# Wide Householder columns: the product with x by TensorE in fp32, panel additions during the wait, no unread streams

## What is computed

```python
# x: (16, 512, 128), adj: (512, 512)
h = einsum('bnd,ed->bne', x, fc_in_w) + fc_in_b
for _ in range(8):                                   # "Euler steps"
    h = h + dt * (alph * 0.5 * (adj @ h - h) + h @ w_eff - h + x)
x = layernorm(x + h)
deg = A.sum(0) + A.sum(1) - diag(A)                  # A = adj
L_norm = rsqrt(deg)[:, None] * (diag(deg) - A) * rsqrt(deg)[None, :]
_, U = eigh(L_norm)
out = relu((U.T @ x) @ W1 + b1) @ W2 + b2
x = layernorm(x + U @ out)
```

## Time and profile before

| | us |
|---|---|
| three runs | 3918.97, 3944.32, 3945.27 |
| median | 3944.32 |
| span of the profiled execution | 3918.1 |

### The profile page before, as it was taken

One profiled execution on the slowest core, in us unless ns is written; L12 is line 12 of the kernel. 1 busy time (PEld: TensorE's weight loads), 2 busy tenths in 40 slices (PEclk: granted clock), 3 DMA queues, 4 the chain that ended last, 5 costly groups with the idle time before them and its releaser, 6 DMA issues.

```text
span 3918.1 us, 62251 instructions
## 1 busy us (share of the span) xinstructions
PE 2790.1 (71%) x13749; PEld 2130.1 (54%) x13749; DVE 3270.7 (83%) x19331; ACT 1093.6 (28%) x4884; POOL 841.7 (21%) x4216
## 2 busy tenths in 40 slices
PE   7999999999999999889999777772123242140088
PEld 6677777777767767667677666662022221020043
DVE  6888999999889888788877777778889999989924
ACT  2333333333333344344444333321000010000013
POOL 3242222222222222233322344440000000000000
PEclk8988999999999999898888655555556566565599
DMA  2000000000000000000000000000000000000001
GB/s 64 1 1 1 1 2 1 1 2 2 1 1 2 1 1 2 1 6 1 1 1 1 1 1 1 1 1 27 1 1 0 0 1 0 0 0 0 0 0 43
DMA packets 14584, 17.39 MB, mean 4 GB/s; under 512 B 1664, under 2 KB 11008, under 8 KB 13952
## 3 DMA queue, kind: packets, MB, share of 16 engines
q1 hardware_dynamic: 14208, 13.42, 1.1%
HBM read 9.22 MB, written 4.19 MB: 3 GB/s over the span
## 4 chain that ended last, share of the span: by engine, by line
DVE 46%; PE 41%; issue 7%; ACT 3%; POOL 3%; DVEq 0%; DMA 0%; POOLq 0%
PE ps L684 10%; PE ps L723 7%; DVE h L2102 4%; PE ps L777 3%; PE ps L640 3%; PE ps L710 3%; PE ps L654 2%; PE ps L662 2%; PE ps L702 2%; DVE small L1613 2%; DVE ps L1597 2%; DVE small L1603 2%; DVE small L1535 2%; PE ps L980 1%; ACT UR L1280 1%
## 5 line engine op out<-in xcount | busy, mean ns | idle before, releaser
L684 PE MATMUL ps<-ident 128*128 128x256 f32 x2992 | 820.9, 414 | 0.0
L684 PEld LDWEIGHTS ps<-ident 128*128 128x128 f32 x2992 | 566.1, 203 | 67.7 <-issue 6.4
L723 PEld LDWEIGHTS ps<-UR 128*128 128x128 f32 x2552 | 378.2, 212 | 195.6 <-DVE UR L1670 93.1
L723 PE MATMUL ps<-UR 128*128 128x41 f32 (+17 forms) x2552 | 390.8, 285 | 95.1 <-ACT UR L1280 69.6
L1068 POOL TENSOR_SCALAR small<-small 128x1 f32<-128x1 f32 x511 | 117.4, 230 | 1227.3 <-ACT small L1244 1209.4
L1242 ACT ACTIVATE small<-ps 128x1 f32<-128x1 f32 x511 | 87.4, 171 | 705.7 <-PE ps L723 705.7
L1264 ACT ACTIVATE small<-lower,small 128x1 f32<-128x1 f32 x383 | 112.9, 295 | 589.3 <-DVE small L1617 589.3
L777 PEld LDWEIGHTS ps<-small,ones 128*128 128x128 f32 x766 | 122.8, 199 | 267.3 <-DVE am L1634 253.7
L702 PE MATMUL ps<-UR,ident 128*128 128x18 f32 (+2 forms) x1020 | 231.6, 309 | 44.3 <-DVE UR L1599 44.3
L1280 ACT ACTIVATE UR<-ident,UR,small 128x1 f32<-128x1 f32 x510 | 197.1, 386 | 99.6 <-POOL small L1077 99.6
L777 PE MATMUL ps<-small,ones 128*128 128x2 f32 x766 | 150.5, 266 | 103.6 <-DVE am L1634 98.1
(11 more groups left out here) (621 smaller groups left out, 7601.7 us busy)
## 6 DMA issues: line engine op xcount, KB each, us to landing
out<-xs SPq DMA_DIRECT2D x16, 256.0 KB, 2.3
m<-in_adj SPq DMA_DIRECT2D x1, 1024.0 KB, 5.4
before<-c_before SPq DMA_DIRECT2D x1, 1024.0 KB, 4.7
notafter<-c_notafter SPq DMA_DIRECT2D x1, 1024.0 KB, 8.2
sib<-c_sib SPq DMA_DIRECT2D x1, 448.0 KB, 3.0
own<-c_own SPq DMA_DIRECT2D x1, 384.0 KB, 3.3
iota<-c_iota SPq DMA_DIRECT2D x1, 256.0 KB, 2.7
h<-c_lanes SPq DMA_DIRECT2D x1, 186.0 KB, 2.4
```

What stands on the lines that cost most here:

```text
L684: nc.tensor.matmul(ps[1][:, 0:2 * P].rearrange("p (a d) -> p a d", a=2), ident[:, 0:P], ident[:, 0:P].unsqueeze(1).broadcast_to([P, 2, P]) ...
L723: last = nc.tensor.matmul(ps[2][:, 0:2 * npend + 3], over(x_of(j)), flat[:, j, 2 * first:2 * k + 3], start=(j == tp), stop=(j == T - 1))
```

## The change

- In wide columns `tile_product` forms the product on TensorE: for each tile m of the result, one fp32 matmul a tile j, with a 128 x 128 block of the matrix as weights and x's one column as the moving operand, summed in `ps[3][:, 16 + m]`. That is `n_on` squared matmuls a column. They stand behind the dots and the s sum; the pivot row goes before the last tile's. `transpose` of x, `row_ready`, VectorE's passes and `y0` go.
- ScalarE copies the products beside VectorE's multiplied pairs, and one reduction (`summed`) gives y. The next matrix column is made in the same way, with its parts copied by ScalarE early, in the time before cy. VectorE writes both halves of the next pair at once (`uc2`, `tcol2`, `pair_masks`), so that ScalarE's two copies at the head of the column go.
- The panel's product is taken over whole tiles into three banks in turn, and VectorE's additions (`panel_rests`) stand just before its wait for the products.
- `keep_clock` keeps two streams at two places in columns 0 to 7 and none from there on. Euler units: one behind cy with four tiles; one behind the products and one behind cy with three tiles outside the panel's columns and with two tiles; one behind cy in the panel's columns with three. So counted, 119 + 208 + 224 = 551, the last in column 366.
- The norms begin at column 390 and come two a column. The table `own` is loaded after the reduction. A, Vt, junk, eye, leafsel and iota become parts of one tensor `big`.
- Narrow columns are a function of their own with the same operations; the pivot row's correction stands ahead of `next_reflected`.

The diff, cut to its core:

```diff
-NORMS_FROM = 292
+NORMS_FROM = 390
-STREAMS = {4: (2, 3, 5), 3: (2, 2, 4), 2: (0, 0, 1), 1: (0, 0, 0)}
-BY_TENSOR = 5
+NORMS_AT_ONCE = 2
...
-            wanted = (1, 0, 1) if n_on > 2 else (0, 1, 1) if n_on == 2 else (0, 0, 0)
-            extra = (0, STREAMS[n_on][place], 0)
+            wanted = (0, 1, 1) if n_on == 2 or n_on == 3 and not panel else (0, 0, 1)
+            extra = (0, 0, 0)
             if k < 8:
+                wanted, extra = (0, 0, 0), (0, 2, 2)
...
+                def tile_product(m):
+                    for j in range(tp, T):
+                        last = nc.tensor.matmul(ps[3][:, 16 + m:17 + m], parts[current[k]][:, j, m * P:(m + 1) * P],
+                                                x_of(j), start=(j == tp), stop=(j == T - 1))
+                    return last
...
                 pe.wait_ge(x_ready, k + 1)
-                if n_on > 1:
-                    for j in range(tp, T):
-                        last = nc.tensor.transpose(ps[0][:, j * P:(j + 1) * P], over(x_of(j)), ident[:, 0:P])
-                    last.then_inc(row_ready, 1)
-                for _ in range(euler_units(k)[0]):
-                    next(state, None)
-                if n_on > 1:
-                    keep_clock(halves_of[k][0])
-                if k <= narrow_from:
-                    pe.wait_ge(xm_ready, k + 1)
-                    if k:
-                        pe.wait_ge(zq_ready, k)
+                if k and k <= narrow_from:
+                    pe.wait_ge(zq_ready, k)
                 if k:
                     pe.wait_ge(u_ready, k)
                 for j in range(tp, T):                      # the dots
...
+                if n_on > 1:
+                    if k:
+                        reflected_product(k - 1)
+                    if switched:
+                        pe.wait_ge(panel_rest, rest_number[first, panel_at[first][2] - 1])
+                    for m in range(tp, T - 1):
+                        tile_product(m)
+                    pivot_row()
+                    tile_product(T - 1).then_inc(products_ready, 1)
...
                 if n_on > 1:
                     pe.wait_ge(y_ready, k + 1)
                     nc.tensor.matmul(ps[3][:, 8:10], ones[:, :], CY, start=True, stop=True).then_inc(cy_ready, 1)
-                    pivot_row()
...
+                        nc.scalar.activation(MBS, pair_masks[:, tp + special, :], ACT.Copy, scale=INVB).then_inc(mb_ready, 1)
+                        act.wait_ge(products_ready, k + 1)
+                        nc.scalar.activation(am[:, 0:n_on * width].rearrange("p (t l) -> p t l", t=n_on)[:, :, 2 * npend:width],
+                                             ps[3][:, 16 + tp:16 + T].unsqueeze(2),
+                                             ACT.Copy).then_inc(product_parts_ready, 1)
                         act.wait_ge(y_done, k + 1)
...
+            def wide_column(k):
+                dve.wait_ge(x_ready, k + 1)
                 if k:
                     next_reflected(k - 1)
+                    reflected_dot(k - 1)
+                inverse = inverse_root(k)
...
+                if npend:
+                    dve.wait_ge(pivot_row_ready, k)
+                    has_column = products(on, n_on, first, npend, ps[4], am[:, 216:432])
+                    h_.wait(has_products)
+                panel_rests(k)
+                dve.wait_ge(product_parts_ready, k + 1)
+                summed(y[:, here], n_on, npend, am[:, 0:216]).then_inc(y_done, 1)
+                dve.wait_ge(y_done, k + 1)
+                h_.post(tt(CY[:, 1:2], y[:, 0:1], ident[:, pp:pp + 1], ALU.mult))
+                h_.sync()
+                stt(out=am[:, 504:504 + n_on], in0=y[:, here], scalar=1.0, in1=x_now,
+                    op0=ALU.mult, op1=ALU.mult, accum_out=CY[:, 0:1]).then_inc(y_ready, 1)
```

More of the change, by code:

```diff
@@ L432, in eig_gnn @@
             n_on, panel = window_of(k)[1], panel_stage(k)
-            place = (0 if panel[1] == 0 else 1 if panel[1] < 2 + panel[4] else 2) if panel else 2
-            wanted = (1, 0, 1) if n_on > 2 else (0, 1, 1) if n_on == 2 else (0, 0, 0)
-            extra = (0, STREAMS[n_on][place], 0)
[L436 to L440, removed]
+            wanted = (0, 1, 1) if n_on == 2 or n_on == 3 and not panel else (0, 0, 1)
+            extra = (0, 0, 0)
             if k < 8:
-                units = (0, 0, 0)
+                wanted, extra = (0, 0, 0), (0, 2, 2)
             left = EULER_UNITS - sum(sum(u) for u in units_of)
[L444 to L447, removed]
+            units_of.append(wanted if left >= sum(wanted) else (0, 0, left))
             halves_of.append(extra)
@@ L452, in euler_units, with norms_at @@
             return units_of[k]
[L454 to L464, removed]
+        SCALES_AT = NORMS_FROM + 2 * T * B // NORMS_AT_ONCE + 4
+        LAST_SCALED = SCALES_AT + 4 + T * B // NORMS_AT_ONCE
+        def norms_at(k, place):
+            if NORMS_FROM <= k < SCALES_AT - 4 or SCALES_AT + 4 <= k < LAST_SCALED:
+                return 1
+            return int(k == SCALES_AT - 4 and place == 0)
         Mrow, AH = before, notafter
@@ L1225, in euler, with pair_mask, panel_copy @@
                             yield
+            def pair_mask(k):
+                tp, n_on, pp = window_of(k)
+                if pp < P - 1:
+                    nc.scalar.activation(pair_masks[:, tp, :], lower[:, pp:pp + 2][:, ::-1], ACT.Copy).then_inc(masks_ready, 1)
+                else:
+                    nc.scalar.activation(pair_masks[:, tp + 1, 0:1], lower[:, 0:1], ACT.Copy).then_inc(masks_ready, 1)
+            def panel_copy(k, what):
+                stage = panel_stage(k)
+                if not stage:
+                    return
+                kb, step, index, t0, n0 = stage
+                i = step - 1
+                if (kb, what, i) not in copied_number:
+                    return
+                cols = slice(t0 * P, N)
+                act.wait_ge(panel_ready, ready_number[kb, i])
+                nc.scalar.activation(panel_rows[i][:, cols], ps[5][0:2 * PANEL, cols], ACT.Copy).then_inc(panel_copied, 1)
@@ L1246, in _ @@
                     nc.scalar.activation(NA[:, 2:5], ps[2][:, 0:3], ACT.Copy).then_inc(root_ready, 1)
[L1247 to L1251, removed]
+                if norms_at(k, 0):
+                    next(norms)
                 if final:
@@ L1462, in _ @@
             for j in range(T):
[L1463 removed]
+                c.post(stt(out=whole[:, j, :], in0=whole[:, j, :], scalar=half[:, j:j + 1],
                            in1=ps[0][:, :], op0=ALU.mult, op1=ALU.mult))
@@ new lines, in _, with products @@
+            h_.post(tt(pairs[:, 0, 0, 0:1], whole[:, 0, 0:1], lower[:, 1:2], ALU.mult))
+            h_.post(stt(out=pairs[:, 0, 0, 1:2], in0=whole[:, 0, 0:1], scalar=lower[:, 0:1], in1=sparks[:, 1, 1:2],
+                        op0=ALU.mult, op1=ALU.add))
+            h_.sync()
+            nc.vector.memset(NOTE, 0.0).then_inc(x_ready, 1)
+            def products(tiles, n_on, first, npend, bank, space):
+                width = 2 * npend + 1
+                swapped = bank[:, 0:2 * npend].rearrange("p (l s) -> p l s", s=2)[:, :, ::-1]
+                mine = space[:, 0:n_on * width].rearrange("p (t l) -> p t l", t=n_on)
+                return h_.mark(tt(mine[:, :, 0:2 * npend].rearrange("p t (l s) -> p t l s", s=2), pairs[:, tiles, first:first + npend, :],
+                                  swapped.unsqueeze(1).broadcast_to([P, n_on, npend, 2]), ALU.mult))
@@ L1527, in reflected_dot @@
                         op0=ALU.mult, op1=ALU.mult, accum_out=SPART).then_inc(z_ready, 1)
-            narrow_from = next(k for k in range(N) if window_of(k)[1] == 1)
-            state = {"panel": 0, "added": 0}
+            state = {"added": 0}
             def half_dot(k):
@@ L1668, in householder @@
                 dve.wait_ge(ucn_ready, k + 1)
-                if not wide_now:
-                    stt(out=pairs[:, tp, k + 1, :], in0=ucN[:, 0:2], scalar=TMP, in1=tcol[:, 0:2],
-                        op0=ALU.mult, op1=ALU.subtract).then_inc(x_ready, 1)
-                    return
                 dve.wait_ge(t_ready, k + 1)
```

444 lines of the change are left out of this document (231 added, 213 removed).

## The result

| | us |
|---|---|
| changed kernel, median of 4 runs | 5383.88 (5374.11 to 5405.14) |
| kernel before, beside it | 3931.64 (3917.99 to 3945.27) |
| ratio, 95% interval | 1.369 (1.3627 to 1.3752) |
| span of the profiled execution | 5378.7 |

The change makes the kernel 37% slower, and 5365 was forecast. The page has VectorE busy 2788 us where it was 3271, and TensorE 4223 where it was 2790. The new product (line 721) is its costliest group; its 7392 weight loads are busy 1581 us, one almost directly behind the other.

A forecast was written before the change was run, and what follows sets the result against it. VectorE's passes over A set the column. Low-clock TensorE products replace them: 3918 + 806 (four tiles) + 475 (three) + 164 (two) = 5363, given as 5365 us; range 4900 to 5600.

The forecast's parts named there:

- The clock: TensorE in wide columns: without streams and with one-column products, the granted clock falls to near 0.50; chance 0.77.
- the first rival: Wide columns keep the full clock: 7.9, 5.8 and 4.7 us a column, 4118 us in all; chance 0.06.
- The price of a record: Each TensorE record, two per fp32 matmul, costs 0.2135 us at the low clock, 0.125 at the full one.
- the rivals: Full clock kept, 4118 us (0.06); mixed clock, about 4740 us (0.12); loads hidden, faster or level, down to 3415 us (0.04).
- A and B: Four-tile column: cy load to next dots, mean 2.0 us; then dots to products, 44 records in order on TensorE, 9.71 us.
- C: Products to cy load, through ScalarE's copy and VectorE's reduction: 1.05, 1.0 and 0.95 us with four, three and two tiles.
- Panel's columns: Panel matmuls, 1.9 us for 480 columns, against 1.3 us of slack: 0.2, 0.1 and 0.1 us a column.
- The clock won back by two units: Columns with two Euler units: full clock 10% of the time in 80 three-tile columns, 30% in 112 two-tile ones.
- What was costed at nothing: Panel additions, one-tile operations, moved norms, ScalarE's tcol activations and the later table load lie under cover and add 0 us.
- The panel additions: VectorE's additions in wide columns lie in the products' shadow: nothing; without that cover at most 44 us.
- the table `own`: Loaded after the reduction, landing in 3.3 us before first need 8 us after the last root: nothing; without cover 3 us.
- VectorE: Its four, three or two passes a wide column leave the chain; it idles before the new reduction, waiting for TensorE's products.

The follow-up runs named there:

- experiment 1: Changed kernel with each new product's moving operand widened from one column: 4288.66 us with 112 columns, 5382.16 with 32, 5234.28 with 64.
- Experiment 2: Kernel before, without unread streams from column 8 on, all else kept: 4445.31 us.
- experiments 1 and 4: The second of the two: changed kernel with four-tile Euler units behind the products instead of behind cy: 5422.4 us, ratio 1.3858.
- experiment 3: Changed kernel with only the diagonal block in each tile's product, 4, 3 and 2 matmuls instead of 16, 9 and 4: 4851.95 us.
- first run of experiment 5: Kernel before, with unread streams in the one-tile stage too, one ahead of the pivot row and two behind cy: 3943.46 us, ratio 1.0067.

## Why the prediction was right, by its steps

The mechanism came out as forecast. That the total lies within 0.4% of 5365 is in part luck: the four- and three-tile stages came out 63 us shorter than forecast and the two-tile stage 74 us longer.

- *The clock.* Right, and what decided: 0.51 to 0.55 in all wide stages, and experiment 1 shows it as the cause. Of the 1452 us lost, 1095 come back when 112 columns move and the rest of the kernel stays; the first rival, the same structure at the full clock, was put at 4118 us and measured at 4289 with a clock of 0.90, 0.94 and 0.85. Experiment 2 shows that taking out the streams is enough to lose much of the clock; the changed kernel with its streams kept was not run, so how much of its low clock is due to them and how much to the new product stays open. By the Trainium skill (TensorE: Matmul & The Clock Gate, section "What's actually happening") the clock follows how busy the engine has been; these runs do not agree if busy means occupied, since TensorE was busy 1514 of 1603 us at 0.51, and they do if it means moving operands.
- *The price of a record.* 0.2135 at the low clock held: 0.213 from one load to the next. At the full clock it is 0.112, not 0.125, and the row of line 600 already said so: the last record's own length was not taken off its 1.03 us, as it had been at the low clock. In the trace of the kernel before, too, the loads of line 600 start 0.111 us apart at the full clock. So it is wrong that no run of records in that trace goes under 0.12 each. This mattered only for the rivals, and 0.112 is still above the 0.098 at which the change would break even.
- *A and B.* 2.0 and 9.71 us were forecast with four tiles. From the ninth column on, the means are 1.6 from the load of cy to the first dot and 9.9 from there to ScalarE's copy. The sum is what counts, since the first dots can start before the others: 11.5 instead of 11.7.
- *C.* 1.05 forecast. It is 1009.49 - 1008.48 = 1.01 in the column above, and 0.99 in the mean off the panel's columns.
- *A slip in the sum.* 12.76 + 0.2 is 12.96 and was written as 12.9; with 12.96 the four-tile stage would have been put at 1646. The mean from the ninth column on is 12.77.
- *Panel's columns.* 0.2 us a column forecast. From the seventeenth column on, the second to sixth of each sixteen take 13.44 us in the mean against 12.58 for the others, which is 0.25 a column over the stage; right in size.
- *The first eight columns.* They have no Euler unit and were costed like the rest. They took 10.3 us each, 20 us less together, and that is most of the -35.
- *The clock won back by two units.* The term that was off. I let the two-tile columns with units run at the full clock for 30% of the time; the profile grants 0.557 in them, which is 11%, and those 112 columns took 6.90 us instead of 6.2: 78 us, all of the +74. The price at the low clock was right: 65 of them ran wholly at it, in 7.22 us against 7.2. In the 80 three-tile columns with two units 10% was assumed and 11% found. I had no row for the share and said so, but took a value a third of the way when the nearest rows all stood at the end. The neighbouring stage that I leaned on had streams besides its units.
- *What was costed at nothing.* The panel additions do lie in the wait. In a two-tile column (timeline) the addition ends before the product's copy comes:

```profile
2906.18 0.41 DVE L1603 TENSOR_TENSOR big<-big,ps 128x256 f32<-128x256 f32 x1
...
2906.82 0.17 ACT L1311 ACTIVATE am<-ps 128x2 f32<-128x2 f32 x1 [0.66 <-PE ps L721]
```

  With the two norms a column the one-tile stage is 2.4 us longer, which is the most that they can have cost. What follows the reduction takes 1274.6 us against 1270.1, but it takes 1268.3 to 1274.6 in the changed kernel and its forms of experiments 1 and 4, and 1269.0 to 1273.7 in the experiments on the kernel before: no cost of the table `own` shows.
- *VectorE.* Its passes went, as did 480 us of its busy time, and it gained idle time only. Even at the full clock the changed column is the longer one: 7.52, 5.72 and 4.95 us (experiment 1) against 6.17, 5.31 and 4.6 in the kernel before, both without a drop. Over the three stages that is an estimated 270 us. So the product in one-column fp32 matmuls loses to VectorE's passes by itself, and the low clock makes the loss about five times as large.

## What to carry to other kernels

Before moving work to TensorE, ask not only how long it will be occupied but what will move through it: one-column products are weight loads, and here the clock stayed at half with 16 or with 4 of them a column (experiment 3). Streams that nobody reads can be worth much in a loop that waits for one short step after another (529 us of 3917 here), so the idle time that they fill is no reason to remove them. Where weight loads set the price, as here, a wider moving operand costs nothing and can hold the clock; that and a few more streams made the kernel before 2.9% faster.

## What the runs showed of the hardware

- Up to 112 columns moved under a weight load of 128 at no cost. The loads of the product start 0.112 us apart at the full clock and 0.213 us at the low one, with 1, 32, 64 and 112 moving columns alike, and the low-clock four-tile stage took 12.6 to 12.7 us a column with 1, 32 and 64.
- How long TensorE is occupied did not decide its clock. It was granted 0.51 while busy 1514 of 1603 us with one-column products, and 0.90 while busy 954 of 1062 us with the same products 112 columns wide.
- The same instructions a column can run at either clock. In the first run of experiment 5 the one-tile loop took about 3.27 us a column at the full clock and 4.7 at the low one, and it stayed at each for 20 us and more at a time. With a product of 256 columns in the same loop the clock stayed full through the stage.
